# Gather passes of a graph network: step addresses as two 16-bit words in place of one 32-bit word

## The chip, the cores and the metric

The kernel runs on one core of one Trainium2 chip. The metric is the time of one execution on the device in microseconds (us), without the profiler; a lower time is better. Three such runs of the kernel before gave 5186.35, 5155.84 and 5162.78 us. The profile is one further execution, taken by the hardware profiler.

## The reference, cut to what matters

50,000 nodes with 64 features and 50,000 edges, sorted by `dst`, go through four layers, each followed by a layer norm:

```
msgs = x[col] * norm[:, None];          out = segment_sum(msgs, row)                 # layer 0
xw = einsum('ni,rih->rnh', x, W);       out = segment_sum(xw[rel, src], dst)         # layer 1
e = silu(silu([h[row], h[col], dist] @ eW1 + eb1) @ eW2 + eb2)
out = silu([h, segment_sum(e, row)] @ nW1 + nb1) @ nW2 + nb2                         # layer 2
h = relu(gcn(x, W1, b1)); out = gcn(h, W2, b2) + x @ W_emb + b_emb                   # layer 3, two sums by dst
```

Everything is float32. Layers 0, 1 and both halves of layer 3 come down to the same work: fetch one row of 64 numbers for every edge, and add it to the row of the edge's target node. `src` is drawn evenly; `dst` is drawn as 50000 times the square of a uniform number, so that the first nodes have many edges and the last ones few.

## The kernel before, in words

The 50,000 edges are padded to 392 tiles of 128, and the nodes to 392 buckets of 128. Two orders of the edges are made by a sort on the chip, one by source (S), one by target (D). The functions run one after the other: `order_sources` (sort S), `stair_pass` e0 with order S (beside it, the sort D is computed), `place_and_relate` (writes order D out), `stair_pass` e1, a node pass, `mlp_pass`, a node pass, `stair_pass` e3, a node pass, `stair_pass` e4, a node pass. The last four sums by target are thus e0, e1, e3 and e4, the **gather passes**.

A gather pass walks a staircase. Since the edges are sorted, a tile of 128 edges touches one bucket or a few neighbouring ones; each of the 784 **steps** (392 + 392) multiplies one tile's messages by a 128x128 one-hot matrix and adds the product to one bucket's 64 columns in PSUM. Which tile and which bucket a step takes is known only at run time, so PE reads both addresses from a table in SBUF into registers. 16 steps are a group (`GS`), and a pass has 49 groups.

- **POOL** (L925) issues one indirect DMA for each tile, 392 in a pass. It gathers 128 rows from HBM into a ring of 128 tiles (`HELD`). It waits when the ring is full, for `s_room`, which SP raises (L940) when PE has finished the groups that used the oldest tiles.
- **DVE** (L977) makes the 16 one-hot matrices of a group in one instruction, two groups deep, reads two numbers of the table of gates (L980, L981), waits for the tiles that have landed and for the PSUM banks that are free, and then raises `s_go` for the group.
- **PE** loads the addresses of a group into registers (L1046), waits for `s_go`, and issues the 16 steps (L1058). A step is a float32 product, and the profile shows it as two weight loads and two matmuls.
- **ACT** (L1092, L1096) copies a finished bank of 8 buckets out and sends it to HBM.

The address table of an order is written by `dve_table`: for each step the tile's place in the ring, shifted left by 6 for its 64 columns, and above it the bucket's place, both in one int32. PE takes them apart with a mask and a shift. The same S table is read once by `mlp_pass` (L1367), which derives from it the table of its own second staircase. The two staircases of `mlp_pass` (L1398 and L1410, L1452 and L1467) have the same form of step, a packed int32 that PE takes apart, and aren't changed. The steps of L1467 are 128 columns wide, those of L1410 and L1058 64.

Of the kernel before, what the change touches and what calls it, by code (L numbers as in the profile page):

```python
# [10 lines left out]
I32 = mybir.dt.int32  # L11
U16 = mybir.dt.uint16
ALU = mybir.AluOpType
# [5 lines left out]
D = 64  # L19
HID = 128  # L20
REL = 8
QUAD = 4
# [18 lines left out]
GS = 16  # L41
GROUPS = 49
STEPS = GS * GROUPS
BL = 8
BH = 49
BANKS = 49
RING = 4
# [6 lines left out]
HELD = 128  # L54
# [7 lines left out]
WHELD = 64  # L62
# [183 lines left out]
class Sorter:  # L246
# [190 lines left out]
    def dve_table(self, dve):  # L437
        nc, K, order = self.nc, self.K, self.order
# [22 lines left out]
        if "halves" in order:  # L461
            expand = order["expand"][:, :]
            self.step(dve, nc.vector.tensor_copy(expand, self.steps_i[:, :]))
            self.step(dve, nc.vector.tensor_scalar(expand, expand, RING * BL - 1, None, ALU.bitwise_and))
            nc.vector.tensor_scalar(expand, expand, 6, None, ALU.logical_shift_left).then_inc(self.sem("pre"), 1)
            self.n += 1
            buckets = order["table"][:, :]
            self.step(dve, nc.vector.tensor_scalar(buckets, self.clipped[:, :], 22, None, ALU.logical_shift_left))
            self.step(dve, nc.vector.tensor_tensor(expand, expand, buckets, ALU.bitwise_or))
            halves = order["halves"][0:1, :, :]  # L470
            half_i = self.steps_i[:, :].rearrange("p (g k) -> p g k", k=HS)
            half_c = self.clipped[:, :].rearrange("p (g k) -> p g k", k=HS)
            nc.vector.tensor_scalar(halves[:, :, 0:1], half_i[:, :, HS - 1:HS], 1.0, None, ALU.add)
            self.step(dve, nc.vector.tensor_scalar(self.clipped[:, :], self.clipped[:, :], 2, None,
                                                   ALU.logical_shift_right))
            nc.vector.tensor_scalar(halves[:, :, 1:2], half_c[:, :, HS - 1:HS], 1.0, None, ALU.add
                                    ).then_inc(self.sem("pre"), 1)
            self.n += 1
            dve.wait_ge(self.sem("pre"), self.n)
        self.step(dve, nc.vector.tensor_scalar(self.clipped[:, :], self.clipped[:, :], 1 if "halves" in order else 3,  # L480
                                               None, ALU.logical_shift_right))
        gates = order["gates"][0:1, :, :]
        rows_i = self.steps_i[:, :].rearrange("p (g k) -> p g k", k=GS)
        rows_c = self.clipped[:, :].rearrange("p (g k) -> p g k", k=GS)
        nc.vector.tensor_scalar(gates[:, :, 0:1], rows_i[:, :, GS - 1:GS], 1.0, None, ALU.add)
        nc.vector.tensor_scalar(gates[:, :, 1:2], rows_c[:, :, GS - 1:GS], 1.0, None, ALU.add)
        self.step(dve, nc.vector.tensor_copy(order["table"][:, :], self.steps_i[:, :]))
        self.step(dve, nc.vector.tensor_scalar(order["table"][:, :], order["table"][:, :], HELD - 1, None,
                                               ALU.bitwise_and))
        self.step(dve, nc.vector.tensor_scalar(order["table"][:, :], order["table"][:, :], 6, None,  # L490
                                               ALU.logical_shift_left))
        self.step(dve, nc.vector.tensor_scalar(self.within[:, :], self.within[:, :], 22, None,
                                               ALU.logical_shift_left))
        nc.vector.tensor_tensor(order["table"][:, :], self.within[:, :], order["table"][:, :], ALU.bitwise_or
                                ).then_inc(self.sem("steps"), 1)

    def dve_payload(self, dve):
        nc, K, place = self.nc, self.K, self.place
# [335 lines left out]
def stair_pass(nc, label, K, order, column, source, sums, fresh=None, sort=None, extra=None, turned=None,  # L834
# [8 lines left out]
    with ExitStack() as ctx:  # L843
# [176 lines left out]
        def _(pe):  # L1020
# [23 lines left out]
                mm.then_inc(s_pextra, 1)  # L1044
            for g in range(GROUPS):
                _, at = nc.values_load_multi_w_load_instructions(  # L1046
                    order["table"][0:1, g * GS:(g + 1) * GS], [mybir.EngineType.PE], min_val=0,
                    max_val=((RING * BL - 1) * D << 16) + (HELD - 1) * D,
                    skip_runtime_bounds_check_because="both parts are masked to their rings before they are stored")
                pe.wait_ge(s_go, g + 1)  # L1050
                for k in range(GS):
                    tile = nc.s_assert_within(
                        at[k] & 0xffff, 0, (HELD - 1) * D,
                        skip_runtime_bounds_check_because="the tile is masked to the ring before it is stored")
                    bucket = nc.s_assert_within(
                        at[k] >> 16, 0, (RING * BL - 1) * D,
                        skip_runtime_bounds_check_because="the bucket is masked to the ring before it is stored")
                    mm = nc.tensor.matmul(ring[:, bass.ds(bucket, D)], hot[g % 2][:, k, :],  # L1058
                                          msgs[:, bass.ds(tile, D)], start=False, stop=False,
                                          skip_group_check=True)  # L1060
                mm.then_inc(s_group, 1)
                if turned is not None and g == 1:
                    for half, (a, b) in enumerate(((0, 4), (4, 7))):
                        for k in range(a, b):
                            mm = flip128(nc, spare[1 + half][0:KS, (k - a) * P:(k - a + 1) * P],
                                         order["keys"][:, k * KS:(k + 1) * KS], K["ident"][:, :])
                        mm.then_inc(s_pkeyt, 1)
                if sort is not None:
                    if 4 <= g < 4 + 3 * PARTS and g % 3 == 1:
                        sort.pe_counts(pe, g // 3 - 1)  # L1070
                    if g == 26:
                        sort.pe_base(pe)
                    if g == 33:
                        sort.pe_steps(pe)
# [72 lines left out]
def mlp_pass(nc, K, order, source, expanded, keyrows, ews, messages, sums, weights):  # L1147
# [5 lines left out]
    with ExitStack() as ctx:  # L1153
# [13 lines left out]
        pairs = region[:, 0:XR * 1024]  # L1167
# [15 lines left out]
        table = region.bitcast(I32)[0:1, later + 12 * QE:later + 12 * QE + STEPS]  # L1183
# [154 lines left out]
        def _(dve):  # L1338
# [10 lines left out]
            for g in range(GROUPS):  # L1349
# [3 lines left out]
                banks = dve.value_load(order["gates"][0:1, g, 1:2], min_val=1, max_val=BANKS)  # L1353
# [5 lines left out]
            for q in range(QUADS):  # L1359
                dve.wait_ge(s_p2, q + 1)  # L1360
                if q >= 2:
# [2 lines left out]
                                        bc(weights["b2"][:, :].unsqueeze(1), [P, QUAD, HID]), ALU.add  # L1364
                                        ).then_inc(s_b2, 1)

            nc.vector.tensor_scalar(table, order["table"][:, :], (WHELD - 1) << 6 | (RING * QUAD - 1) << 22, None,  # L1367
                                    ALU.bitwise_and).then_inc(s_table, 1)
            dve.wait_ge(s_table, 1)
            nc.vector.tensor_scalar(table, table, 1, None, ALU.logical_shift_left).then_inc(s_table, 1)  # L1370
# [9 lines left out]
            for g in range(GROUPS):  # L1380
                if g + 1 < GROUPS:
                    one_hots(g + 1)
                for e in (2 * g, 2 * g + 1):
                    tiles = dve.value_load(order["halves"][0:1, e, 0:1], min_val=1, max_val=T)
                    banks = dve.value_load(order["halves"][0:1, e, 1:2], min_val=1, max_val=QUADS)
# [897 lines left out]
def gnn(nc, x, src, dst, rel, ew, W, eW1, eb1, eW2, eb2, nW1, nb1, nW2, nb2, W1, b1, W2, b2, We, be, out):  # L2283
# [24 lines left out]
    with ExitStack() as ctx:  # L2308
        def sb(name, shape, dt=F32):
            return ctx.enter_context(nc.sbuf_tensor(name, shape, dt))  # L2310
# [7 lines left out]
        def semaphore(name):  # L2318

            if name not in semaphores:  # L2320
# [13 lines left out]
        K["ending"] = sb("ending", [1, BATCHES])  # L2334
        orders = {n: {"index": {c: sb(f"index_{n}{c}", [P, T], I32) for c in columns}, 
                      "used": sb(f"used_{n}", [1, 64], U16), "keys": sb(f"keys_{n}", [P, STEPS]),
                      "table": sb(f"table_{n}", [1, STEPS], I32), "gates": sb(f"gates_{n}", [1, GROUPS, 2], U16), "banks": sb(f"banks_{n}", [1, 64], U16)}
                  for n, columns in (("S", (0, 2)), ("D", (0, 2)))}
        orders["S"]["halves"] = sb("halves", [1, 2 * GROUPS, 2], U16)
        orders["S"]["half_banks"] = sb("half_banks", [1, BANKS, 2], U16)  # L2340
# [90 lines left out]
```

## Time and profile before

| | us |
|---|---|
| median of three runs | 5162.78 |
| lowest and highest run | 5155.84, 5186.35 |
| span of the profiled execution, first to last instruction | 6462.1 |
| profiled execution over the median | 1299.3 |

| engine | busy us | share of the span |
|---|---|---|
| PE (matmul) | 3919.6 | 61% |
| POOL | 2886.1 | 45% |
| DVE | 2177.2 | 34% |
| ACT | 1422.3 | 22% |

The profiled execution was a quarter longer than the runs; its own time isn't given apart from its span. All times of stretches and instructions below are from it. A busy time counts matmuls, weight loads and the work of the other engines. Register instructions of PE aren't counted as busy: they appear only in the view of one source line, on an engine named PEldq, as ALU_OP, FUSED_REGOPS and TENSOR_LOAD. Idle time "<-issue" is time in which the engine waited for nothing that the profile shows. The granted clock is given as a share of 2.4 GHz: 0.50 is 1.2 GHz.

### The profile page before, as it was taken

What the parts mean: (1) busy time and instruction counts of PE and PEld (TensorE: products, weight loads), DVE (VectorE), ACT (ScalarE), POOL (GpSimd) and SP (SyncE); (2) the same over time, 40 slices, a digit from 0 to 9 for tenths busy, and PEclk for the clock granted to TensorE, in tenths of its full rate; (3) what the DMA queues carried; (4) which work ended last, traced back from release to release, by engine and by line L of the source; (5) the groups of instructions that cost most, each with busy time, mean ns of one, the idle gap of its engine ahead of it and who ended that gap; (6) DMA issues with size and microseconds to landing.
All of it is one profiled execution on the core that took longest, in us unless ns stands there. A gap on an engine that the chain in (4) does not pass through costs nothing. (4 is left out here: it accounts for less than half of the span.)

```text
span 6462.1 us, 74448 instructions
## 1 busy us (share of the span) xinstructions
PE 3919.6 (61%) x19983; PEld 3086.7 (48%) x19983; DVE 2177.2 (34%) x4653; ACT 1422.3 (22%) x3080; POOL 2886.1 (45%) x2799
## 2 busy tenths in 40 slices
PE   3333451668656742667466759888952669626697
PEld 2122121667422322666265646776732668426586
DVE  7444790324645620124311102343530112102134
ACT  0000000001333420112200126443420223302135
POOL 2555406663566766661555540000146660366602
PEclk8555575555666765555555569999975555755569
DMA  3000131111445641223734436554631222412235
GB/s 99 2 2 2 47 113 33 43 42 42 155 175 202 234 153 38 66 70 138 264 99 101 107 116 202 181 180 181 227 113 35 69 69 84 145 36 69 69 106 177
DMA packets 354959, 692.13 MB, mean 107 GB/s; under 512 B 183337, under 2 KB 185254, under 8 KB 339130
## 3 DMA queue, kind: packets, MB, share of 16 engines
q1 hardware_dynamic: 148381, 491.73, 21.7%
q10 hardware_dynamic: 118428, 130.12, 6.0%
q0 software_dynamic: 87808, 66.01, 5.8%
q8 instruction: 182, 2.98, 0.2%
q14 instruction: 160, 1.30, 0.1%
HBM read 350.87 MB, written 349.58 MB: 108 GB/s over the span
## 5 line engine op out<-in xcount | busy, mean ns | idle before, releaser
L1058 PE MATMUL e_ring<-e_msgs,e_hot 128*128 x6272 | 1419.4, 413 | 1091.3 <-issue 1082.7
L1058 PEld LDWEIGHTS e_ring<-e_msgs,e_hot 128*128 128x128 f32 x6272 | 1385.0, 328 | 1127.4 <-issue 1125.9
L925 POOL DMA_INDIRECT e_msgs<-y,index_D x784 | 741.4, 946 | 640.9 <-POOLq L77 261.1
L977 DVE TENSOR_TENSOR e_hot<-e_nodes,keys_D 128x2048 f32<-128x2048 f32 x147 | 336.9, 2292 | 1596.9 <-remote 872.0
L599 POOL DMA_INDIRECT list_D<-d_place,d_target x392 | 456.2, 1164 | 326.6 <-DVEq L553 210.5
L925 POOL DMA_INDIRECT e_msgs<-y,index_S x392 | 396.8, 1012 | 387.7 <-DVE index_S L963 198.3
L599 POOL DMA_INDIRECT list_S<-s_place,s_target x392 | 390.6, 996 | 362.8 <-DVEq L553 247.5
L1241 POOL DMA_INDIRECT m_far<-x,index_S x392 | 390.9, 997 | 347.9 <-DMA pairs_by_edge<-m_far 221.4
L1410 PE MATMUL m_ring<-m_region,m_hot 128*128 x1568 | 375.9, 426 | 215.7 <-issue 213.3
L925 POOL DMA_INDIRECT e_msgs<-x_by_relation,index_D x392 | 374.0, 954 | 210.4 <-issue 112.8
L1410 PEld LDWEIGHTS m_ring<-m_region,m_hot 128*128 128x128 f32 x1568 | 348.1, 328 | 244.3 <-issue 242.2
L2086 POOL TENSOR_TENSOR n_sq<-n_cent 128x1792 f32<-128x1792 f32 x14 | 44.4, 3175 | 837.0 <-DVE n_cent L1981 837.0
L1096 ACT ACTIVATE e_stage<-e_ring,dinv 128x64 f32<-128x64 f32 x784 | 171.6, 330 | 1078.5 <-DMA pairs_by_edge<-m_stage 475.6
L804 PE MATMUL s_p_deg<-s_hot_low,s_hot_high 128*128 128x392 f16 x784 | 256.0, 473 | 160.0 <-DVE s_hot_low L709 152.0
L1745 PE MATMUL d_p_w<-wall,d_xt 64*128 64x512 f32 x784 | 300.8, 808 | 80.9 <-DVE d_stage L1704 55.6
L1092 ACT COPY e_stage<-e_ring 128x512 f32<-128x512 f32 x98 | 57.4, 586 | 1211.1 <-remote 903.4
L2099 POOL TENSOR_TENSOR n_out<-n_cent,n_rstd 128x1792 f32<-128x1792 f32 x28 | 89.4, 3192 | 453.0 <-DVE n_rstd L1991 453.0
L1467 PE MATMUL m_ring<-m_region,m_hot 128*128 x1568 | 227.7, 303 | 59.6 <-issue 52.0
L1467 PEld LDWEIGHTS m_ring<-m_region,m_hot 128*128 128x128 f32 x1568 | 214.6, 190 | 72.7 <-issue 68.6
L1345 DVE TENSOR_SCALAR m_hot<-m_keyrow,slots 128x2048 f32<-128x2048 f16 x49 | 63.3, 1292 | 515.0 <-remote 280.1
L977 DVE TENSOR_TENSOR e_hot<-e_nodes,keys_S 128x2048 f32<-128x2048 f32 x49 | 112.2, 2290 | 341.9 <-remote 242.1
L522 DVE SCALAR_TENSOR_TENSOR s_scratch<-s_p_k,low_src,before 128x128 bf16<-128x128 f32 x392 | 113.6, 344 | 334.6 <-remote 303.4
(368 smaller groups left out, 5846.1 us busy)
## 6 DMA issues: line engine op xcount, KB each, us to landing
x_by_relation<-d_stage SPq DMA_DIRECT2D x98, 1024.0 KB
agg<-e_stage ACTq DMA_DIRECT2D x196, 256.0 KB
n_in<-agg SPq DMA_DIRECT2D x42, 896.0 KB, 5.6
x<-n_out SPq DMA_DIRECT2D x28, 896.0 KB, 3.6
m_keyrow<-keys_by_step SPq DMA_DIRECT2D x49, 512.0 KB
m_region<-pairs_by_edge SPq DMA_DIRECT2D x49, 512.0 KB
messages<-m_region SPq DMA_DIRECT2D x98, 256.0 KB
m_region<-messages SPq DMA_DIRECT2D x49, 512.0 KB, 4.1
```

The source lines that it names most:

```text
L522: op = self.nc.vector.scalar_tensor_tensor(out=self.scratch[:, h, j, :], in0=of[:, j, :], scalar=self.low[:, t:t + 1], in1=self.K["before" ...
L599: pool.indirect_dma_start(out=self.listing, out_offset=bass.IndirectOffsetOnAxis(ap=self.target[:, t:t + 1], axis=0), in_=self.place[:, t, ...
L804: mm = nc.tensor.matmul(p_deg[m // QUADS][:, 0:T], hot_high[m % 2][:, j, :], hot_low[m % 2][:, j, :], start=q == 0 and j == 0, stop=q == Q ...
L925: pool.indirect_dma_start(out=msgs[:, (i % HELD) * D:(i % HELD + 1) * D], out_offset=None, in_=source, in_offset=bass.IndirectOffsetOnAxis ...
L977: nc.vector.tensor_tensor(hot[g % 2][:, :, :], bc(nodes[:, 0:P].unsqueeze(1), [P, GS, P]), bc(order["keys"][:, g * GS:(g + 1) * GS].unsque ...
L1058: mm = nc.tensor.matmul(ring[:, bass.ds(bucket, D)], hot[g % 2][:, k, :], msgs[:, bass.ds(tile, D)], start=False, stop=False, skip_group_c ...
L1096: nc.scalar.activation(stage[r][:, k * D:(k + 1) * D], ring[:, at:at + D], ACT.Identity, scale=scale[:, m * BL + k:m * BL + k + 1]).then_i ...
L1241: pool.indirect_dma_start(out=far[:, (i % AHEAD) * D:(i % AHEAD + 1) * D], out_offset=None, in_=source, in_offset=bass.IndirectOffsetOnAxi ...
L1410: mm = nc.tensor.matmul(ring[:, bass.ds(tile, D)], hot[g % HOTS][:, k, :], region[:, bass.ds(bucket, D)], start=False, stop=False, skip_gr ...
L1467: mm = nc.tensor.matmul(ring[:, bass.ds(bucket, HID)], hot[g % HOTS][:, k, :], msgs[:, bass.ds(tile, HID)], start=False, stop=False, skip_ ...
L1745: nc.tensor.matmul(p_w[m % NW][:, :], xt[w % 2][half:half + D, k // 2, :], wall[half:half + D, :], start=True, stop=True).then_inc(s_pw, 1)
L2099: nc.gpsimd.tensor_tensor(result[0][h][:, :, :], cent[h][:, :, :], bc(rstd[h][:, :].unsqueeze(2), [P, CH, D]), ALU.mult).then_inc(s_done, 1)
```

## The change: what it does

The table of an order becomes `pairs`, with two 16-bit words for each step, the tile's place and the bucket's. `dve_table` writes each of the two into its half with a converting copy. PE loads 32 words for a group instead of 16, and uses the registers as they are: the mask and the shift go. The space in SBUF is the same, and scratch use of the table as int32, and `mlp_pass`, go through a view of the same bytes.

```diff
@@ dve_table, order S only
-            buckets = order["table"][:, :]
+            buckets = order["pairs"][0:1, :, :].rearrange("p s c -> p (s c)").bitcast(I32)
@@ dve_table
-        nc.vector.tensor_scalar(gates[:, :, 1:2], rows_c[:, :, GS - 1:GS], 1.0, None, ALU.add)
-        self.step(dve, nc.vector.tensor_copy(order["table"][:, :], self.steps_i[:, :]))
-        self.step(dve, nc.vector.tensor_scalar(order["table"][:, :], order["table"][:, :], HELD - 1, None,
-                                               ALU.bitwise_and))
-        self.step(dve, nc.vector.tensor_scalar(order["table"][:, :], order["table"][:, :], 6, None,
+        self.step(dve, nc.vector.tensor_scalar(gates[:, :, 1:2], rows_c[:, :, GS - 1:GS], 1.0, None, ALU.add))
+        pairs, tile = order["pairs"][:, :, :], self.clipped
+        self.step(dve, nc.vector.tensor_copy(tile[:, :], self.steps_i[:, :]))
+        self.step(dve, nc.vector.tensor_scalar(tile[:, :], tile[:, :], HELD - 1, None, ALU.bitwise_and))
+        self.step(dve, nc.vector.tensor_scalar(tile[:, :], tile[:, :], 6, None, ALU.logical_shift_left))
+        nc.vector.tensor_copy(pairs[:, :, 0], tile[:, :]).then_inc(self.sem("pre"), 1)
+        self.n += 1
+        self.step(dve, nc.vector.tensor_scalar(self.within[:, :], self.within[:, :], 6, None,
                                                ALU.logical_shift_left))
-        self.step(dve, nc.vector.tensor_scalar(self.within[:, :], self.within[:, :], 22, None,
-                                               ALU.logical_shift_left))
-        nc.vector.tensor_tensor(order["table"][:, :], self.within[:, :], order["table"][:, :], ALU.bitwise_or
-                                ).then_inc(self.sem("steps"), 1)
+        self.step(dve, nc.vector.tensor_copy(pairs[:, :, 1], self.within[:, :]))
+        nc.vector.sem_inc(self.sem("steps"), 1)
@@ stair_pass, PE
-                    order["table"][0:1, g * GS:(g + 1) * GS], [mybir.EngineType.PE], min_val=0,
-                    max_val=((RING * BL - 1) * D << 16) + (HELD - 1) * D,
+                    order["pairs"][0:1, g * GS:(g + 1) * GS, :].rearrange("p s c -> p (s c)"), [mybir.EngineType.PE],
+                    min_val=0, max_val=(HELD - 1) * D,
...
                     tile = nc.s_assert_within(
-                        at[k] & 0xffff, 0, (HELD - 1) * D,
+                        at[2 * k], 0, (HELD - 1) * D,
...
                     bucket = nc.s_assert_within(
-                        at[k] >> 16, 0, (RING * BL - 1) * D,
+                        at[2 * k + 1], 0, (RING * BL - 1) * D,
@@ mlp_pass, DVE
-            nc.vector.tensor_scalar(table, order["table"][:, :], (WHELD - 1) << 6 | (RING * QUAD - 1) << 22, None,
+            packed = order["pairs"][0:1, :, :].rearrange("p s c -> p (s c)").bitcast(I32)
+            nc.vector.tensor_scalar(table, packed, (WHELD - 1) << 6 | (RING * QUAD - 1) << 22, None,
```

PE, the start of the first group of pass e0, before. ISA is the instruction that the trace calls FUSED_REGOPS, REGISTER_ALU the one that it calls ALU_OP:

```order
L72 MATMUL e_spare<-ident,e_entry 98x128 x4
L1046 TENSOR_LOAD table_S
L1058 REGISTER_ALU
L1058 ISA
L1058 MATMUL e_ring<-e_msgs,e_hot 128x64
L1058 REGISTER_ALU
```

The same place after the change:

```order
L72 MATMUL e_spare<-ident,e_entry 98x128 x4
L1047 TENSOR_LOAD pairs_S
L1059 ISA
L1059 MATMUL e_ring<-e_msgs,e_hot 128x64
L1059 ISA
```

One REGISTER_ALU for each step is gone, 3136 in the four passes: PE's list falls from 17201 rows to 14065. The FUSED_REGOPS stays, and so does one TENSOR_LOAD for each group (196 in all), which now fills 32 registers instead of 16.

DVE, the end of `dve_table` for order D, before:

```order
L487 CAST table_D<-e_steps_i 1x784
L488 TENSOR_SCALAR table_D<-table_D 1x784
L490 TENSOR_SCALAR table_D<-table_D 1x784
L492 TENSOR_SCALAR e_within<-e_within 1x784
L494 TENSOR_TENSOR table_D<-e_within,table_D 1x784
```

And after:

```order
L488 CAST e_clipped<-e_steps_i 1x784
L489 TENSOR_SCALAR e_clipped<-e_clipped 1x784
L490 TENSOR_SCALAR e_clipped<-e_clipped 1x784
L491 CAST pairs_D<-e_clipped 1x784
L493 TENSOR_SCALAR e_within<-e_within 1x784
L495 CAST pairs_D<-e_within 1x784
```

Two converting copies stand where one TENSOR_TENSOR stood, once for each order: one instruction more each time. POOL, SP and ACT issue the same instructions as before.

## Rows read from the trace of the kernel before

**Rows 1.** The page's granted clock of PE in 40 equal slices, tenths of 2.4 GHz

```profile
PEclk8555575555666765555555569999975555755569
```

**Rows 2.** Waits of PE over the span: engine line <- releaser: us, times, longest

```profile
PE e_ring L1058 <- issue: 1082.7, 597, 7.8
PE m_ring L1410 <- issue: 213.3, 139, 9.7
```

**Rows 3.** Line L1058, whole span: engine op xcount: ns min/median/max, first to last start

```profile
L1058 PEldq ALU_OP  x3136: 2/32/1397, 966.5 to 6235.6; - x196
L1058 PEldq FUSED_REGOPS  x3136: 2/84/1394, 966.6 to 6235.7; - x196
```

**Rows 4.** Line L1058 from 2370 to 2548 us, the ring of pass e1 filling

```profile
L1058 PEldq FUSED_REGOPS  x44: 84/699/710, 2369.8 to 2544.2; - x44
L1058 PEldq ALU_OP  x43: 7/692/709, 2371.2 to 2544.1; - x43
```

**Rows 5.** Line L1058 from 2924 to 2999 us, after POOL's last issue in e1

```profile
L1058 PE MATMUL e_ring<-e_msgs,e_hot x354: 421/421/421, 2923.7 to 2999.0; 128*128 x177
L1058 PEldq FUSED_REGOPS  x176: 80/84/84, 2924.0 to 2998.7; - x176
L1058 PEldq ALU_OP  x175: 32/32/32, 2924.3 to 2998.6; - x175
```

**Rows 6.** Stretches: busy us and instructions of each engine, PEclk, DMA share, GB/s

```profile
core 0: us, PE busy (x) PEld busy (x) DVE busy (x) ACT busy (x) POOL busy (x), PEclk, DMA share, GB/s
2370.00:2548.00 178.00, 24.71 (x83) 22.52 (x83) 4.58 (x2) 1.18 (x2) 121.13 (x127) 0.50 0.13 27
2590.00:2900.00 310.00, 188.69 (x849) 186.91 (x849) 61.30 (x27) 31.74 (x54) 202.55 (x214) 0.50 0.26 67
2924.00:2999.00 75.00, 75.00 (x354) 75.00 (x353) 25.21 (x11) 12.93 (x22) 0.00 (x0) 0.50 0.19 64
...
4120.00:4380.00 260.00, 209.04 (x1447) 196.58 (x1447) 103.12 (x45) 106.97 (x182) 0.00 (x0) 1.00 0.56 175
```

**Rows 7.** Waits from 2590 to 2900 us

```profile
PE e_ring L1058 <- issue: 122.2, 80, 2.9
POOL e_msgs L925 <- issue: 60.7, 199, 0.3
POOL e_msgs L925 <- SPq L940: 47.1, 15, 3.4
```

**Rows 8.** Line L925, POOL's gathers, whole span, pass e1

```profile
L925 POOL DMA_INDIRECT e_msgs<-x_by_relation,index_D x392: 949/955/1018, 2348.8 to 2907.4; - x196
```

**Rows 9.** Line L1467 from 4201.3 to 4205.5 us, one group of the unchanged staircase

```profile
L1467 PEldq ALU_OP  x15: 32/32/32, 4201.3 to 4205.3; - x15
L1467 PEldq FUSED_REGOPS  x15: 92/94/94, 4201.4 to 4205.4; - x15
```

**Rows 10.** Register loads by line, whole span: PE's of 16, DVE's of one

```profile
L1046 PEldq TENSOR_LOAD <-table_D x147: 8/1106/1511, 2351.7 to 6229.2; - x147
L1452 PEldq TENSOR_LOAD <-m_region x49: 1102/1270/1497, 4104.2 to 4383.5; - x49
L980 DVEq TENSOR_LOAD <-gates_D x147: 281/285/439, 2357.8 to 6226.4; - x147
```

**Rows 11.** Line L1046 from 2932.8 to 2939 us, one load in the tail of e1

```profile
L1046 PEldq TENSOR_LOAD <-table_D x1: 1102/1102/1102, 2933.7 to 2933.7; - x1
```

**Rows 12.** Timeline of DVE there: start us, us, engine line op, idle before, releaser

```profile
2930.96 2.29 DVE L977 TENSOR_TENSOR e_hot<-e_nodes,keys_D 128x2048 f32<-128x2048 f32 x1 [4.54 <-PE e_ring L1058]
2937.78 2.29 DVE L977 TENSOR_TENSOR e_hot<-e_nodes,keys_D 128x2048 f32<-128x2048 f32 x1 [4.53 <-PE e_ring L1058]
```

**Rows 13.** DVE's instructions on the table of order S

```profile
L487 DVE CAST table_S<-s_steps_i x1: 549/549/549, 736.0 to 736.0; 1x784 int32<-1x784 f32 x1
L494 DVE TENSOR_TENSOR table_S<-s_within,table_S x1: 961/961/961, 738.4 to 738.4; 1x784 int32<-1x784 int32 x1
```

More of the change, by code:

```diff
@@ L2336, in gnn @@
                       "used": sb(f"used_{n}", [1, 64], U16), "keys": sb(f"keys_{n}", [P, STEPS]),
-                      "table": sb(f"table_{n}", [1, STEPS], I32), "gates": sb(f"gates_{n}", [1, GROUPS, 2], U16), "banks": sb(f"banks_{n}", [1, 64], U16)}
+                      "pairs": sb(f"pairs_{n}", [1, STEPS, 2], U16), "gates": sb(f"gates_{n}", [1, GROUPS, 2], U16), "banks": sb(f"banks_{n}", [1, 64], U16)}
                   for n, columns in (("S", (0, 2)), ("D", (0, 2)))}
```

## The prediction, made blind

> **What bounds the kernel now.** I read the granted clock and the waits of PE first, then line L1058 (the step of a gather pass), then pass e1 in three stretches.
>
> The waits name PE's own issue as the largest loss: 1082.7 us of idle time before the matmuls of L1058 and 213.3 us before those of L1410, all "<-issue" [rows 2]. That looks like a sequencer that can't keep up, and each step has two register instructions on it [rows 3]. The stretches say when this is so. While the ring of e1 fills, from 2370 to 2548 us, POOL issues gathers without a pause and PE gets 83 matmuls through in 178 us; a register instruction lasts 0.69 us there [rows 4, 6]. From 2590 to 2900 us, PE is idle for 122.2 us on issue, and POOL, which is ahead by the whole ring, waits 47.1 us for room [rows 7]. From 2924 to 2999 us, after POOL's last issue at 2907.4 us, PE is busy for 75.00 of 75 us, and the same two register instructions take 32 and 84 ns [rows 5, 6, 8]. The stall is tied to POOL's issuing, and there it is twenty times the work of the instruction.
>
> **Is that stall in the runs?** The profiled span is 6462.1 us and the median 5162.78 us, 1299.3 us less. The idle time on issue before L1058 and L1410 is 1082.7 + 213.3 = 1296.0 us [rows 2]. That the two agree so well is partly chance, since other work also gets shorter or longer, but no other group of rows offers 1300 us. I take the stall as something that recording adds, and that the runs don't have. The Trainium skill (NOTIFIC — the notification-queue block, section on overflow) says that the block which writes such records holds up its producers when it can't take more; by it alone no size follows, and no run here shows it.
>
> Without that stall, pass e1 has three rates to compare:
> - POOL: 0.955 us for a gather [rows 8] and 60.7/199 = 0.305 us ahead of it [rows 7], 1.26 us for a tile, 392 x 1.26 = 494 us.
> - PE's array at the low clock: in the tail 75 us for 354 matmuls, two for a step, 0.424 us for a step [rows 6]; 784 x 0.424 = 332 us.
> - PE's sequencer: the unchanged staircase of L1467 has the same pattern (one ALU_OP, one FUSED_REGOPS, two loads and two matmuls) at a granted clock of 1.00 [rows 6], where the array doesn't cover it. There 15 ALU_OPs start within 4.0 us [rows 9], 4.0/14 = 0.286 us for a step, and the load of a group comes on top with 1.27 us [rows 10]: 784 x 0.286 + 49 x 1.27 = 286 us.
>
> So in the runs a pass should go by POOL (494 us), then by the array (332 us), and the sequencer comes last. In the order by target the late tiles touch more buckets: with targets at the square of a uniform number, the last tiles need about three steps each, 3 x 0.424 = 1.27 us, which is POOL's rate again and still the array's, not the sequencer's. Even if POOL is some 15% faster without the recorder, the array follows, at 1.2 GHz. The change touches the third rate only.
>
> **The change, part by part.** The sum is against the profiled execution's own span where it uses its rows, and I carry the difference over to the median, since the stall that the two differ by is taken out.
>
> 1. *3136 ALU_OPs go.* On PE's sequencer one takes at least its own 32 ns [rows 9] and at most what a step has beside FUSED_REGOPS, 0.286 - 0.092 = 0.19 us. Shared evenly, the rest of a step (0.286 - 0.032 - 0.092 = 0.162 us over six instructions) adds 0.027, so 0.059 us is my value, 185 us in all; the ends are 3136 x 0.032 = 100 and 3136 x 0.19 = 596 us. All of it lies beside the array: in the tail PE has no idle time at all between matmuls with both instructions in place [rows 6], and earlier PE waits for tiles. Booked: 0. If the cover is gone, 185 us.
> 2. *196 loads fill 32 registers instead of 16.* A load of one register takes 0.285 us and of sixteen 1.106 us [rows 10] (the first is DVE's, the nearest row), so (1.106 - 0.285)/15 = 0.055 us a register, and 16 more are 0.88 us: 1.98 us. It is 172 us in all; at worst it doubles, 217 us. The cover: the load in the tail starts at 2933.7 us [rows 11], and the group that is then in the array ends at 2937.8, when DVE is let into the next one-hot matrices [rows 12]. PE's sequencer is thus 4.1 us ahead, and a load of up to some 3.8 us stays hidden. Where PE waits for tiles, the load stands ahead of the wait in the program and is hidden too. Booked: 0.
> 3. *DVE:* a TENSOR_TENSOR of 0.961 us is replaced by two copies of 0.549 us [rows 13] in each of two orders, 2 x (1.098 - 0.961) = +0.3 us. The strided two-byte writes aren't in the trace; at twice the price of a copy this would be +2.5 us. For order S it is on the path, for order D beside e0.
> 4. *PE's clock* stays at 0.50 in the passes [rows 1, 6], the tail's 75 us without idle time included. Fewer register instructions can't make PE busier than that.
>
> Sum: 0 + 0 + 0.3. Forecast **5163 us**, no change.
>
> The Trainium skill (TensorE: Matmul & The Clock Gate, Part 1) says that sustained activity lifts the array to 2.4 GHz. The trace disagrees here: 75.00 of 75 us busy at 0.50 [rows 6]. By the rule, the groups after POOL's last issue would run at the sequencer's rate, and the sum would hold the saving of point 1 for them; that is rival B.
>
> **The rivals.**
>
> *A, faster: part of the stall is the kernel's own.* Where POOL issues, PE's instructions are slow whatever they do, and one of six for a step is gone. For it: the stall begins and ends with POOL's gathers [rows 4, 5]. Against it: all of it can't be there, as the runs are 1299 us shorter. With all of the 1082.7 us real, a sixth is 180 us: 4983 us. With a third real it is 60 us: 5103 us. Chance 0.17, of which 0.14 beyond 1%.
>
> *B, about even or faster: the array at 2.4 GHz and PE the bound.* Then the sequencer sets the rate as in L1467: -185 us for the ALU_OPs, +172 us for the loads, which are then open, net -13 us, 5150 us; the ends are -596 + 172 = -424 us and -100 + 172 = +72 us. Against it: the clock in rows 6, and POOL's 494 us, which would have to fall below 286. Chance 0.09, of which 0.06 faster by over 1%.
>
> *C, slower: the load of 32 registers is open.* The array starves at each group's edge. It decides from 3.8 us a load, 0.17 us for each of the further 16 registers, or earlier if PE without the recorder is less far ahead than 4.1 us. Then the 196 loads cost their growth, 172 to 217 us, and nothing comes back for the ALU_OPs, which the array hides: 5335 to 5380 us; if only the 14 groups after POOL's last issue are hit, 56 x 0.88 = 49 us, 5212 us. The Trainium skill (Runtime: NRT & Kernel Launch, Instruction fetch mechanics) prices such a load at about 200 ns a register, which would make 6.4 us of 32 and put 2.3 us or more in the open for each group. By that figure a load of 16 would take 3.2 us; the trace has 1.106 [rows 10]. Chance 0.06, for slower by over 1%: 0.05.
>
> That the change doesn't do what it says is excluded by the order of instructions: the ALU_OPs are gone, the loads are not more in number.
>
> **Numbers.** Forecast 0.68, A 0.17, B 0.09, C 0.06. A measurement of this kernel can tell about 1% (52 us) from no change; the three runs lie within 0.6%. Faster by over 1%: 0.14 + 0.06 = 0.20. Slower: 0.05. Within 1%: 0.75. Range: 5060 us (A with a bit over half of the stall real, 103 us) to 5200 us (the forecast, with the runs' own spread of 24 us above the median and points 2 and 3 at their worst in some groups). It leaves out about 0.12 below and 0.06 above.
>
> **What would show it.** In the profile after: no ALU_OP on the step's line; TENSOR_LOAD near 2.0 us (over 3.8 speaks for C); in the tail of each pass still no idle time and groups 6.8 us apart [rows 12], so that the tail is no shorter; PEclk still 0.50 (1.00 speaks for B). The profiled span itself should fall by 100 to 250 us, since the recorded stall is by instruction (1082.7/6 = 180 us); a profiled span that falls while the runs don't is what the forecast stands on. Wrong it is if the runs fall by 60 us or more: then the stall or the sequencer was in the runs, and the agreement of 1296 with 1299 us was chance.

## The result

The change makes the kernel slower by 4.6%: the ratio to the kernel before is 1.046, 95% interval 1.042 to 1.050. The forecast of no change was wrong, and the time lies above its range.

| | runs | median us | lowest to highest us |
|---|---|---|---|
| before | 4 | 5173.91 | 5155.84 to 5186.35 |
| after | 4 | 5410.61 | 5408.65 to 5432.14 |

The profiled execution of the changed kernel has a span of 5406.6 us, as long as its runs. That is 1055.5 us shorter than the profiled execution of before, on which the prediction was worked out, although the kernel is slower. The two profiles can't be set against each other as they stand; experiment e6 gives the profile of before that belongs beside it.

### The profile page after: what moved, and what is told of

Its sections match the earlier page's. It is cut to its first block and busy times, and to the rows that moved or that the text cites. A ratio compares the mean times of both kernels' runs of the same rounds, so it can differ in the third digit from the quotient of the medians.

```text
span 5406.6 us, 71316 instructions
## 1 busy us (share of the span) xinstructions
PE 3717.6 (69%) x19983; PEld 2991.5 (55%) x19983; DVE 2176.2 (40%) x4655; ACT 1416.6 (26%) x3080; POOL 2915.0 (54%) x2799
## 5 line engine op out<-in xcount | busy, mean ns | idle before, releaser
L1059 PE MATMUL e_ring<-e_msgs,e_hot 128*128 x6272 | 1388.7, 423 | 834.8 <-issue 781.1
L1059 PEld LDWEIGHTS e_ring<-e_msgs,e_hot 128*128 128x128 f32 x6272 | 1352.8, 332 | 872.5 <-issue 872.5
L600 POOL DMA_INDIRECT list_S<-s_place,s_target x392 | 407.6, 1040 | 213.4 <-issue 118.5
L1242 POOL DMA_INDIRECT m_far<-x,index_S x392 | 404.5, 1032 | 130.5 <-issue 113.1
L805 PE MATMUL s_p_deg<-s_hot_low,s_hot_high 128*128 128x392 f16 x784 | 239.6, 448 | 184.4 <-DVE s_hot_low L710 184.2
L1412 PE MATMUL m_ring<-m_region,m_hot 128*128 x1568 | 342.2, 422 | 20.3 <-DVEq L1358 16.6
L1747 PE MATMUL d_p_w<-wall,d_xt 64*128 64x512 f32 x784 | 231.1, 711 | 79.4 <-DVE d_stage L1706 77.3
L1469 PE MATMUL m_ring<-m_region,m_hot 128*128 x1568 | 227.7, 303 | 59.7 <-issue 52.3
L805 PEld LDWEIGHTS s_p_deg<-s_hot_low,s_hot_high 128*128 128x128 f16 x784 | 75.3, 117 | 307.2 <-DVE s_hot_low L710 252.4
L1774 ACT COPY d_stage<-d_p_w 128x512 f32<-128x512 f32 x294 | 161.1, 589 | 172.0 <-PE d_p_w L1747 166.2
```

Source lines behind the costliest of these rows:

```text
L600: pool.indirect_dma_start(out=self.listing, out_offset=bass.IndirectOffsetOnAxis(ap=self.target[:, t:t + 1], axis=0), in_=self.place[:, t, ...
L805: mm = nc.tensor.matmul(p_deg[m // QUADS][:, 0:T], hot_high[m % 2][:, j, :], hot_low[m % 2][:, j, :], start=q == 0 and j == 0, stop=q == Q ...
L1242: pool.indirect_dma_start(out=far[:, (i % AHEAD) * D:(i % AHEAD + 1) * D], out_offset=None, in_=source, in_offset=bass.IndirectOffsetOnAxi ...
L1412: mm = nc.tensor.matmul(ring[:, bass.ds(tile, D)], hot[g % HOTS][:, k, :], region[:, bass.ds(bucket, D)], start=False, stop=False, skip_gr ...
L1469: mm = nc.tensor.matmul(ring[:, bass.ds(bucket, HID)], hot[g % HOTS][:, k, :], msgs[:, bass.ds(tile, HID)], start=False, stop=False, skip_ ...
L1747: nc.tensor.matmul(p_w[m % NW][:, :], xt[w % 2][half:half + D, k // 2, :], wall[half:half + D, :], start=True, stop=True).then_inc(s_pw, 1)
```

## The profile after

The step's line is L1059 now, and the register load L1047. Views of one line, columns as in [rows 3]:

```profile
L1059 PE MATMUL e_ring<-e_msgs,e_hot x6272: 421/421/471, 651.7 to 5184.5; 128*128 x196
L1059 PEldq FUSED_REGOPS  x3136: 55/55/65, 651.6 to 5180.5; - x196
...
L1047 PEldq TENSOR_LOAD <-pairs_D x147: 7520/7968/8277, 1864.9 to 5169.8; - x147
L1047 PEldq TENSOR_LOAD <-pairs_S x49: 7701/7947/10532, 643.6 to 1229.0; - x49
```

The ALU_OP is gone, as planned, and the remaining FUSED_REGOPS is shorter, 55 ns instead of 84 [rows 3]. The load of a group takes 7.97 us, where that of before took 1.106 [rows 10]. The prediction had 1.98 us for it.

Waits of PE over the span, the row that answers to [rows 2], and then two stretches of pass e1 (columns as in [rows 6]): one while POOL gathers, one after its last issue at 2354.4 us:

```profile
PE e_ring L1059 <- issue: 781.1, 185, 7.1
```

```profile
1900.00:2300.00 400.00, 254.10 (x1149) 247.50 (x1148) 82.50 (x36) 42.32 (x72) 303.34 (x318) 0.50 0.28 73
2360.00:2419.00 59.00, 38.33 (x175) 37.42 (x175) 9.17 (x4) 5.28 (x9) 0.00 (x0) 0.50 0.07 27
```

In both stretches PE is busy for 64 or 65% of the time. In the second one nothing is left to wait for but its own sequencer, and the tail of before had 75.00 of 75 us busy there [rows 6]. From 1900 to 2300 us a load starts every 11.18 us (median): 7.96 us are the load, 0.06 us later the first step's FUSED_REGOPS starts, 2.74 us after that the last one, and 0.43 us later the next load. No wait for DVE's signal is left between them. Of the 16 steps the first thirteen start 0.13 us apart and the last ones 0.43 us, the array's time for a step; that makes the group about 1.0 us longer for the sequencer than sixteen quick steps would. The timeline of the second stretch shows one group after another (start us, us, engine line operation):

```profile
2368.76 6.82 PE L1059 MATMUL e_ring<-e_msgs,e_hot 128*128 x31
...
2375.61 2.29 DVE L978 TENSOR_TENSOR e_hot<-e_nodes,keys_D 128x2048 f32<-128x2048 f32 x1 [8.87 <-PE e_ring L1059]
...
2380.00 7.09 PE L1059 MATMUL e_ring<-e_msgs,e_hot 128*128 x32 [4.42 <-issue]
2387.12 2.29 DVE L978 TENSOR_TENSOR e_hot<-e_nodes,keys_D 128x2048 f32<-128x2048 f32 x1 [9.22 <-PE e_ring L1059]
...
2391.14 1.11 PE L1059 MATMUL e_ring<-e_msgs,e_hot 128*128 x4 [4.05 <-issue]
```

A group starts at 2380.00 us and the next at 2391.14, 11.1 us apart, of which the array works 7.1; DVE is let on 11.5 us apart. The rest, 4.0 to 4.4 us, is what the load has beyond the work still queued for the array. In the tail of before a group came every 6.8 us [rows 12].

## The experiments

The kernel before took one of two times. e1 to e4 ran on one chip in one session and e8 to e11 on another; on both it took 6449 us. e5 to e7 and e12 with e13 ran on two more, on which it took 5174 and 5175 us. No chip was used in two sessions, so chip and session aren't told apart; "chip" below stands for both. "The stall" is the slow register instructions and the idle time on issue of [rows 2, 4]. Ratios are always to runs of the kernel before on the same chip.

| run | what is different from the kernel before | us | ratio, 95% interval |
|---|---|---|---|
| e1 | nothing | 6448.54 | 1.001 (0.998 to 1.003) |
| e2 | pairs of 32-bit words, order D | 6442.53 | 1.000 (0.998 to 1.002) |
| e3 | 8 of 16 steps by 16-bit words | 6500.53 | 1.009 (1.006 to 1.011) |
| e4 | 12 of 16 steps by 16-bit words | 6603.24 | 1.024 (1.021 to 1.027) |
| e5 | the change | 5431.4 | 1.048 (1.044 to 1.053) |
| e6 | nothing | 5180.4 | 1.003 (0.999 to 1.007) |
| e7 | 32-bit pairs, order D and second staircase of `mlp_pass` | 5137.34 | 0.993 (0.990 to 0.997) |
| e8 | as e3 | 6490.8 | 1.006 (1.003 to 1.009) |
| e9 | as e4 | 6607.13 | 1.024 (1.021 to 1.027) |
| e10 | 32-bit pairs, second staircase of `mlp_pass` only | 6392.31 | 0.992 (0.990 to 0.995) |
| e11 | 32-bit pairs, order D, fetched with a stride | 6626.94 | 1.028 (1.025 to 1.031) |
| e12 | as e4 | 5190.58 | 1.001 (0.998 to 1.005) |
| e13 | as e3 | 5174.1 | 0.999 (0.996 to 1.002) |

### e1: the kernel before, again

No edit.

> The kernel before, unchanged, once more with a profile. Theory 'single execution': the profiled execution of 6462.1 us was one of its own, the stalls on issue belong to it, and this profile has a span near the runs (about 5170 us), register instructions of 32 and 84 ns also where POOL issues, and gather passes that go by POOL: in pass e1 from POOL's first issue to the last matmul 494 us and a tail of 10 to 30 us. Rival 'recording': whoever records this kernel gets the stall, the span is near 6460 us again, and only fewer register instructions make it go away. The time without profile is 5160 to 5190 us by both.

The time without the change was already 6448.54 us, and all 28 runs of this kernel on that chip lay between 6421 and 6483 us. The last sentence of the expectation fell: the stall isn't only in a profile. Its rows are back:

```profile
PE e_ring L1058 <- issue: 1073.6, 584, 8.3
PE m_ring L1410 <- issue: 216.1, 150, 10.9
```

So neither "one odd execution" nor "recording alone" is right as it was put. On this chip every timed run is as long as a profile with the stall.

### e2: words of 32 bits instead of 16

The declaration of the table, set against the one of the changed kernel (shortened). To make room, the constant `after` is kept elsewhere in SBUF:

```diff
-                      "pairs": sb(f"pairs_{n}", [1, STEPS, 2], U16)
+                      "pairs": sb("pairs_D", [1, STEPS, 2], I32)     # order D; order S keeps the packed table
```

> In the three passes of order D the two addresses stand as two 32-bit words (32 registers of 32-bit words for a group, no mask and shift); order S stays packed, with the mask and the shift. Theory 'width': what costs 7.9 us is that each 16-bit word is fetched by itself at about 0.25 us; then this load takes 1.98 us (0.055 us a register), the sequencer needs about 2.0 + 3.2 = 5.2 us for a group, less than the array's 6.8 and POOL's 10.1, and the time is that of before, ratio 0.995 to 1.005. Rival 'count': more than 16 registers make the load slow, whatever their width; then it takes about 7.9 us again, the three passes go at 11.2 us a group, and the ratio is about 1.033.

The load of 32 registers, line L1062 of this kernel:

```profile
L1062 PEldq TENSOR_LOAD <-pairs_D x147: 2127/2408/2609, 2330.8 to 6182.4; - x147
```

It takes 2.13 to 2.41 us, near the 1.98 that the prediction had extrapolated, and the ratio is 1.000. "Count" is refuted: as many registers, a quarter to a third of the load. What made 8 us of it is how the 16-bit words are fetched. And 147 groups without the mask and the shift bring nothing that can be measured, with the stall present: the passes of order D took 640.5 to 641.4 us in this profile and 642.6 to 644.9 in e1's.

### e3 and e4: half and three quarters by 16-bit words

The table is the changed kernel's, since its bytes read as one 32-bit word are the packed table of before. Only the loads and the use of their registers differ (e3; e4 has 12 for 8, and 24 for 16; `load` stands for the long call):

```diff
+                words = order["pairs"][0:1, g * GS:(g + 1) * GS, :].rearrange("p s c -> p (s c)")
+                both = words.bitcast(I32)
+                _, halves = load(words[:, 0:16])      # 16-bit words of steps 0 to 7
+                _, at = load(both[:, 8:GS])           # packed words of steps 8 to 15
...
-                        at[2 * k], 0, (HELD - 1) * D,
+                        halves[2 * k] if k < 8 else at[k - 8] & 0xffff, 0, (HELD - 1) * D,
-                        at[2 * k + 1], 0, (RING * BL - 1) * D,
+                        halves[2 * k + 1] if k < 8 else at[k - 8] >> 16, 0, (RING * BL - 1) * D,
```

> In all four passes the first 8 steps of a group take 16-bit words (16 registers), the last 8 the packed 32-bit words of the same bytes with mask and shift (8 registers), in two loads. Theory 'width': 16 x 0.25 = 4.0 us for the first load and about 0.7 us for the second. The sequencer needs 4.7 + 0.2 + 8 x 0.19 + 8 x 0.28 = 8.7 us for a group. Theory 'rate' (a pass goes by the slowest of POOL 10.1, sequencer, array 6.8 us a group): 8.7 is below 10.1, so at most the late groups of order D, which have fewer tiles, get longer; ratio 1.00 to 1.012. Theory 'lead' (all of a load beyond 3.8 us is open in each group): 0.9 us x 196 = 176 us, ratio 1.034. By 'count' both loads are short (1.1 and 0.7 us) and the ratio is 1.00.

> As the half, but 12 of the 16 steps take 16-bit words (24 registers) and 4 packed ones. Theory 'width': 24 x 0.25 = 6.0 us and about 0.45 us, and the sequencer needs 6.45 + 0.2 + 12 x 0.19 + 4 x 0.28 = 10.1 us for a group, just POOL's rate on average: late groups of order D are open, early ones hidden, ratio 1.015 to 1.035. Theory 'lead': 2.65 us x 196 = 520 us, ratio 1.10. By 'count' (slow beyond 16 registers) the first load is slow as well, by a share that this theory doesn't give.

The loads of e3, of 16 words of 16 bits (L1049) and of 8 packed ones (L1052):

```profile
L1049 PEldq TENSOR_LOAD <-pairs_D x147: 996/3797/4260, 2352.3 to 6250.1; - x147
...
L1052 PEldq TENSOR_LOAD <-pairs_D x147: 586/591/700, 2356.2 to 6254.0; - x147
```

"Width" holds: 3.80 us for sixteen, 0.237 us a word, as expected. The ratios 1.009 and 1.024 are below what "lead" gives (1.034 and 1.10) and fit "rate". But on this chip POOL isn't the bound between the stalls, so they don't yet say from what length on a load costs time there.

### e5 and e6: change and before, side by side on a third chip

> The changed kernel, once more, beside the kernel before on the same chip. In the last runs the kernel before took about 6450 us on its chip and not 5170, with the stall of its profile, so the state goes with the chip or the session. Theory 'width and rate': the load takes 7.9 us in any state, the sequencer needs 11.2 us for a group, and the kernel is slower than before by 190 to 260 us where the kernel before takes 5170 us (ratio 1.04 to 1.05), and by 200 to 320 us where it takes 6450 us, since the first half and the three quarters of 16-bit words cost 51 and 154 us there (ratio 1.03 to 1.05). Rival 'fewer instructions lift the stall': the changed kernel takes 5410 us also where the kernel before takes 6450, and would be faster there (ratio 0.84).

> The kernel before, unchanged, for its profile on the chip of this call. If the time is near 5170 us: no stall in the profile, register instructions of 32 and 84 ns also where POOL issues, POOL's last gather of pass e1 494 us after its first, the last matmul 10 to 30 us later, and four gather passes that are together 190 to 260 us shorter than in the changed kernel. If it is near 6450 us: the same picture as the last time.

Here the kernel before took 5173.88 us and the changed one 5431.4 us. "Fewer instructions lift the stall" can't be tested where there is none, but e2 to e4, e10 and e11 kept it with fewer of them. The changed kernel itself was not run on a chip with the stall, so what it costs there isn't shown. The profile of before without the stall (e6, span 5178.7 us):

```profile
L1058 PEldq ALU_OP  x3136: 32/32/42, 663.4 to 4954.5; - x196
L1058 PEldq FUSED_REGOPS  x3136: 80/84/102, 663.5 to 4954.6; - x196
...
L1046 PEldq TENSOR_LOAD <-table_D x147: 1101/1105/1118, 1795.0 to 4943.4; - x147
...
L925 POOL DMA_INDIRECT e_msgs<-x_by_relation,index_D x392: 947/952/1017, 1792.1 to 2283.2; - x196
```

```profile
PE e_ring L1058 <- DVEq L985: 578.0, 193, 8.6
...
L977 DVE TENSOR_TENSOR e_hot<-e_nodes,keys_D 128x2048 f32<-128x2048 f32 x147 | 336.9, 2292 | 1105.9 <-SPq L943 1099.5
```

```profile
1850.00:2250.00 400.00, 285.99 (x1292) 278.66 (x1293) 93.97 (x41) 46.98 (x80) 303.05 (x319) 0.50 0.30 79
```

No register instruction of a step lasts longer than 102 ns, and PE's waits end at DVE's signal (L985). DVE's own idle time before L977, 1105.9 us, ends for 1099.5 us of it at SP's count of the tiles that have landed (L943). So PE waits for tiles: from the end of a load to the first step it is 4.74 us (median, 1850 to 2250 us), where the changed kernel has 0.06. POOL's gathers of pass e1 start within 491.1 us (2283.2 - 1792.1) and issue 319 in 400 us, one in 1.25 us, as the prediction had it. Over 49 groups that is 10.0 us a group. Pass e1 from the first to the last matmul, here and in the changed kernel (first profile of it):

```profile
L1058 PE MATMUL e_ring<-e_msgs,e_hot x1568: 420/421/472, 1807.0 to 2294.1; 128*128 x196
```

```profile
L1059 PE MATMUL e_ring<-e_msgs,e_hot x1568: 421/421/471, 1877.1 to 2420.1; 128*128 x196
```

487.1 against 543.0 us, 55.9 us more. Pass e0 goes from 510.0 to 592.1 us (663.6 to 1173.6, and 651.7 to 1243.8), 82 us more. There the sort's matmuls stand in PE's program between groups: from a group's last step to the next load it is 1.4 us on average and not 0.43. Before the change the sequencer's wait for tiles had room for this work (4.2 us a group on average in e0 of e6); now it comes on top of the load. The four passes of e6 add up to 1966.4 us and those of e5 to 2221.0 us: 254.6 us more, of a difference of 257.1 us between the two spans (5435.8 - 5178.7). The loss is in the gather passes, to within 3 us.

### e7 and e10: 32-bit pairs where PE's sequencer is the bound

Two more DVE instructions take the table of the second staircase of `mlp_pass` apart, and PE loads 32 neighbouring words of 32 bits for a group (cut to one of the two uses):

```diff
+            nc.vector.tensor_scalar(wide[:, :, 0], table, 0xffff, None, ALU.bitwise_and).then_inc(s_table, 1)
+            nc.vector.tensor_scalar(wide[:, :, 1], table, 16, None, ALU.logical_shift_right).then_inc(s_table, 1)
...
-                        at[k] & 0xffff, 0, (WHELD - 1) * HID,
+                        at[2 * k], 0, (WHELD - 1) * HID,
```

> 32-bit pairs for the three passes of order D, as in the run before, and also for the second staircase of mlp_pass (L1467), the one place where the clock is 1.00 and PE's sequencer is the bound: two more DVE instructions make its table, the load of a group grows from 1.27 us to about 2.3 us, and 16 ALU_OPs for a group go. Theory 'an ALU_OP is worth its place on the sequencer' (0.09 us between its start and that of the instruction behind it): 16 x 0.09 = 1.4 us less and 1.0 us more for a group, 49 x 0.4 = 20 us less: the staircase takes 260 us instead of 280. Rival 'an ALU_OP costs 0.03 us or less': 0.5 us less and 1.0 us more for a group, the staircase takes 305 us. Against the kernel before the whole is 0.995 to 1.005 by both.

> The gather passes as in the kernel before; only the second staircase of mlp_pass takes 32-bit pairs without the mask and the shift. In the run that had both, that staircase fell from 279.6 to 242.2 us and the gather passes stayed. So all of the gain is here: 34 to 40 us less, ratio 0.992 to 0.994 where the kernel before takes 5170 us. The rival is that the 32-bit pairs of order D gave part of it: then this is 0.995 or more.

The second staircase of `mlp_pass` before (e6, L1467, with its load L1452):

```profile
L1467 PE MATMUL m_ring<-m_region,m_hot x1568: 274/278/574, 3153.0 to 3432.6; 128*128 x196
...
L1452 PEldq TENSOR_LOAD <-m_region x49: 1109/1280/1495, 3147.2 to 3426.7; - x49
```

And in e7 (L1488, L1473):

```profile
L1488 PE MATMUL m_ring<-m_region,m_hot x1568: 274/275/574, 3158.3 to 3400.5; 128*128 x196
L1488 PEldq FUSED_REGOPS  x784: 64/64/79, 3158.2 to 3399.1; - x196
...
L1473 PEldq TENSOR_LOAD <-m_region x49: 2130/2482/3043, 3153.8 to 3394.2; - x49
```

From 279.6 to 242.2 us, 37.4 us less, more than the 20 us expected: a group is 0.76 us shorter although its load is 1.20 us longer, so 16 steps give back 1.97 us, 0.123 us for each. Part of it is the FUSED_REGOPS, 64 instead of 94 ns. e10, with this edit alone, on a chip with the stall, has a ratio like that of e7 (0.992 against 0.993) and a second staircase of 242.4 us. The pairs of order D add nothing: passes e1, e3 and e4 took 488.1, 484.4 and 484.5 us in e7 and 487.1, 484.6 and 484.6 in e6, although the load of those passes grew from 1.105 to 2.131 us. Both versions are 0.7 to 0.8% faster than the kernel before; e10 needs the smaller edit.

### e11: the same 32-bit words, not neighbours

Two loads for a group, each of every second word (shortened):

```diff
+                    parts = [load(order["pairs"][0:1, g * GS:(g + 1) * GS, c]) for c in range(2)]    # 32-bit, order D
```

> As the 32-bit pairs of order D, but a group's tiles and buckets are fetched by two loads of 16 words each, every second word, so that the 32-bit words aren't neighbours. Theory 'width': only the width of a word counts, each load takes 1.1 us, 2.2 together, no change. Theory 'neighbours': a load fetches neighbouring words together, at 0.055 us each, and single words at 0.25 us, and 16-bit words always singly; then each load takes 4.0 us, 8.0 together, the order D passes go at about 11.2 us a group and take 543 us instead of 485, ratio 1.034. No run so far tells these two apart.

```profile
L1062 PEldq TENSOR_LOAD <-pairs_D x294: 3787/3797/4448, 2337.1 to 6395.3; - x147
```

3.797 us for 16 words of 32 bits with a word between them: to the nanosecond the median of 16 words of 16 bits in e3. "Width" alone falls, "neighbours" stands. The times are as if a load fetched neighbouring 32-bit words together, and strided ones and 16-bit ones each by itself; what the hardware does inside a load no run shows. The kernel is slower by 2.8%, with passes of order D of 707 us, where e1 and e10 have 643 to 646. That the same long loads cost time again, with 32-bit words and no 16-bit ones, ties the loss to the length of the load.

### e8, e9, e12 and e13: how a long load reaches the end

The kernels are those of e3 (e8, e13) and e4 (e9, e12).

> The first 8 steps of a group by 16-bit words, the last 8 packed, once more, for a chip where the kernel before takes about 5170 us. There the kernel before goes at 9.9 to 10.0 us a group, POOL's rate; this one took 7.7 to 7.9 us a group in its tails, where POOL had ended. Theory 'rate' (a pass goes by the slowest engine): 7.8 is below 9.9, no change, ratio 0.998 to 1.004. Theory 'lead' (what a load has beyond 3.8 us is open at each group's edge): the loads take 3.8 + 0.6 = 4.4 us, 0.6 us x 196 = 118 us, ratio 1.023. If the chip is one where the kernel before takes 6450 us: 1.0085 again.

> 12 of 16 steps by 16-bit words, once more, for a chip where the kernel before takes about 5170 us. In its tails it took 9.3 to 9.6 us a group. Theory 'rate': still below POOL's 9.9 to 10.0, little or no change, ratio 1.000 to 1.008; the step to the changed kernel (11.2 us a group, ratio 1.048) is then a threshold and not a slope. Theory 'lead': 5.7 + 0.3 - 3.8 = 2.2 us x 196 = 431 us, ratio 1.083. A plain slope through 0 of 16 and 16 of 16 steps: three quarters of 257 us, ratio 1.037.

e8 and e9 fell on a chip with the stall and repeated e3 and e4 (1.006 and 1.024).

> 12 of 16 steps by 16-bit words (9.3 to 9.6 us a group in its tails). Where the kernel before takes about 5170 us, theory 'rate' has it still below POOL's 9.9 to 10.0 us a group: ratio 1.000 to 1.008. Theory 'lead': 1.083. A plain slope between the kernel before and the changed one: 1.037. Where the kernel before takes 6450 us: 1.024 again, and the question stays open.

> 8 of 16 steps by 16-bit words (7.7 to 7.9 us a group in its tails). Where the kernel before takes about 5170 us, theory 'rate': 0.998 to 1.004; theory 'lead' 1.023; plain slope 1.024. Where it takes 6450 us: 1.006 to 1.009 again.

Without the stall, three quarters of the steps by 16-bit words cost nothing that can be measured, 1.001 (0.998 to 1.005), although the loads take 6.0 us together:

```profile
L1049 PEldq TENSOR_LOAD <-pairs_D x147: 5660/5669/5903, 1789.3 to 4926.8; - x147
...
L1052 PEldq TENSOR_LOAD <-pairs_D x147: 327/333/670, 1795.1 to 4932.5; - x147
```

```profile
L1064 PE MATMUL e_ring<-e_msgs,e_hot x1568: 421/421/472, 1801.4 to 2288.8; 128*128 x196
```

Pass e1 takes 487.4 us in e12, as in e6; there is still some wait between a load and its first step (0.64 us, median). Half of the steps (e13) cost nothing either, 0.999 (0.996 to 1.002). "Lead" had 1.083 for it and a plain slope 1.037; "rate" is the one that holds. The loss starts between 6.0 us of load in a group and 7.97 on a chip without the stall. With it, the 4.4 us of e3 and e8 already cost 0.6 to 0.9%.

## Why the prediction was wrong

**The failed step is point 2 of the change**, "196 loads fill 32 registers instead of 16": 0.88 us more a load, at worst 1.1. It was 6.86 us more. The price per register was taken from a load of sixteen neighbouring 32-bit words [rows 10] and carried over to 16-bit words, for which the trace of before had only loads of a single word. That single word (0.285 us) was in the row, and read as a fixed cost; 32 times it is 9.1 us, much nearer the truth than 1.98. With bounds from the nearest rows on both sides, the load would have reached from 2 to 9 us and rival C would have had a real chance instead of 0.06. The Trainium skill (Runtime: NRT & Kernel Launch, Instruction fetch mechanics) has about 200 ns a register, for loads from HBM; by an estimate from that figure, 32 registers take 6.4 us. I dismissed it because 16 packed words took 1.106 us and not 3.2. e3 and e11, whose tables are in SBUF, come within a fifth of it (0.237 us a register against 0.2), and e7, with 2.13 us for 32 neighbours of 32 bits, doesn't.

**Rival C was the right case, with the wrong way of counting.** It had the load open in each group beyond 3.8 us. By that, 7.97 us would cost (7.97 - 3.8) x 196 = 817 us; the four passes lost 254.6. What decides is the rate of each part over a whole group. PE's sequencer needs 7.97 us for the load and the rest of the 11.1 us, about 3.2, for the 16 steps; POOL needs 10.0; the array 6.8. Before the change POOL was the slowest, after it the sequencer, and the difference is what is paid: (11.1 - 10.0) x 49 = 54 us a pass, measured 55.9 in e1. The prediction's 3.8 us of cover for a load was about right, since the array stands still for 4.0 to 4.4 us in a group and the load has 4.2 beyond that cover. But that idle time is set against an array that needs 6.8 us where POOL leaves it 10.0, and so 3.2 us of it in each group cost nothing.

**Points 1 and 3 held.** In the gather passes the ALU_OPs are worth nothing (order D: e2 with the stall, e7 without it). Rival A, which had a sixth of the stall go with them, falls by e2. Their price where the sequencer is the bound was set at 0.059 us and is 0.123 us with what the FUSED_REGOPS gains, still within the ends of 0.03 and 0.19. DVE's copies into 16-bit words took 0.625 and 0.739 us; they change nothing that shows.

**Point 4 held.** The granted clock is 0.50 in both stretches after the change, with PE busy for 64 and 65% of the time, as it was in the tail of before with PE busy throughout [rows 6].

**That the stall isn't in the runs was right for the runs shown, for a reason that fell.** I took it as something that recording adds. e6 is recorded and has none; e1 to e4 and e8 to e11 are slow in all timed runs. It goes with the chip or the session. That 1296 us came so near to 1299 [rows 2] was chance, as e6 shows. Without the stall the idle time before L1058 falls only from 1091.3 to 578.8 us, since PE then waits for tiles instead. The four gather passes take 1966.4 us in e6 and 2605.0 in the profile of before, 639 us less, and the first staircase of `mlp_pass` (L1410) 354.3 and 581.5, 227 less. Most of the rest, 303 and 91 us, lies ahead of e0 (`order_sources`) and between e0 and e1 (`place_and_relate`), which the prediction didn't look at. The stall is not twenty times the work of both instructions either: that is the ALU_OP (692 against 32 ns), and for the FUSED_REGOPS it is eight times [rows 4, 5]. What holds up PE's register instructions there, while POOL issues gathers [rows 4, 5], stays open; no experiment was aimed at it.

**Late tiles don't touch more buckets.** The prediction gave the last tiles of order D three steps each. A bucket of this kernel is one column of the node layout, every 392nd node, not 128 neighbours, so the skew of `dst` is spread over all of them. In e6 PE starts 320 matmuls in 100 us early in pass e1 and 332 late:

```profile
1850.00:1950.00 100.00, 70.86 (x320) 69.03 (x320) 22.92 (x10) 11.75 (x20) 75.91 (x80) 0.50 0.30 79
2150.00:2250.00 100.00, 73.06 (x332) 71.22 (x332) 24.65 (x11) 11.75 (x20) 75.86 (x80) 0.50 0.28 74
```

The sum didn't rest on it.

## What to carry to other kernels

Before an instruction is traded for a wider load, price the load by its own form: word size, neighbours or not, count. A row for another form gives one end of a range, and the load of one word times the count gives the other. Then compare the engines' rates over a whole group; a cost below the slowest engine's slack is free, and above it only the excess is paid. Take the profile from an execution as long as the runs; a profile a quarter longer shows other bounds. The same kind of trade made a gain of 0.8% in the staircase where the sequencer is the bound and the words are 32-bit neighbours.

## What the runs showed of the hardware

- A register load on PE: 4 neighbouring 32-bit words 0.333 us (e12), 8 words 0.591 (e3), 16 words 1.105 (e6), 32 words 2.13 (e7; 2.41 in e2, with the stall), 0.064 us for each further word. 16-bit words: 16 in 3.797 us (e3), 24 in 5.669 (e12), 32 in 7.97 (changed kernel), 0.24 to 0.25 us a word. 32-bit words with a stride of two: 16 in 3.797 us (e11).
- A step without the ALU_OP starts 0.13 us after the one before it on PE's sequencer for the first thirteen steps of a group, and 0.43 us after it, the array's pace, for the last ones (changed kernel, pass e1).
- The kernel before took 5174 and 5175 us on two chips and 6449 us on two others, 25% more, each in one session. The longer time comes with register instructions of up to 1.4 us while POOL issues indirect DMAs [rows 3], against 102 ns at most in e6. Ratios between kernels differ between the two kinds of chip (three quarters by 16-bit words: 1.001 and 1.024), so a profile should come from the chip whose times are to be explained. What sets the two kinds apart stays open.
